# Rounding projected key blocks on ScalarE from PSUM instead of on VectorE from SBUF

## The chip, the cores and the metric

The kernel runs on one core of a Trainium2 chip. The metric is the device time of one execution in microseconds, from launch to end. The engines are called TensorE (PE in the profile; PEld is its weight load), VectorE (DVE), ScalarE (ACT), GpSimd (POOL) and SyncE (SP, which here only issues DMAs).

## What is computed

A layer norm, then causal attention with 16 heads plus a mixture of nine experts of which each token uses two, both added to the input. Cut to the attention, in which the change lies:

```
xn  = layernorm(x)                                  # x: 2 x 1024 x 128
K   = einsum('bpd,ihd->biph', xn, W_K)              # 16 heads of 64
Q   = einsum('bpd,ihd->biph', xn, W_Q)
V   = einsum('bpd,ihd->biph', xn, W_V)
s   = where(tril, einsum('biph,biqh->biqp', K, Q), -1e10)
z   = einsum('biph,biqp->biqh', V, softmax(s / 8))
out = x + einsum('bqf,df->bqd', z_flat, W_O) + moe(xn)
```

## The kernel before, in words

**Exactness.** TensorE multiplies in the type fp32r. To keep the accuracy of fp32, an operand is held as two fp32r tiles: the rounded value ("hi") and the remainder ("lo", the value less hi). A product is then two or three matmuls that accumulate. So nearly every matmul result goes through the same mill: ScalarE copies the PSUM bank into hi (a copy to an fp32r tile rounds), VectorE subtracts hi from the bank and writes lo.

**Stages.** The first 142 us hold the layer norm, the routing and the experts. Then come the attention's 16 halves: 8 pairs of heads (p), and for each the two sequences of the batch (b = 0, 1). A half has 16 score units, one for each head of the pair and each 128-row block of queries, in the order of `UNITS`: unit 0 has 1024 columns of keys, unit 1 has 128, unit 2 has 896, and so on. For each unit n these steps follow one another:

- S n, on PE (line 1390): scores into one half of `ps_big`, which two units share in turn. S n waits for the exponential of unit n-2.
- X n, on DVE (line 1109): the mask and the row's maximum.
- E n, on ACT (line 853): the exponential into `probs`, with its sum, which a short second instruction (the accumulator read) delivers. Its end releases the bank.
- R n, on DVE (line 1147): the reciprocal of the sum. N n, on POOL (line 693): the division.
- T n.g, on PE (line 1422): transposes of up to four tiles into one of the two banks of `ps_mid`. H n.g, on ACT (line 866), makes hi of it, and L n.g, on DVE (line 1158), lo. T of a group waits for L of the group two before it.
- V, on PE (lines 1442 and 1443): probabilities times values into `ps_z` or `ps_big`, and Z, the moves and sums of that result.

**Projections.** While a half runs, the queries and keys of the next half are projected, and in 7 of the 15 halves that have a successor the values too. Each projection is an M on PE (lines 1252 to 1254) and a C on ACT and on DVE. All of them use one PSUM bank, `ps_misc`: an M waits until the previous user has read the bank. They come in the order k0, q0, q1, k1, then the values v0, v2, v3 where they are made, then the output product o1, and so on; k0 and k1 are the first and second 512 keys.

**Key blocks before the change.** For k0 and k1 (there are 30 such blocks in all, two in each of 15 halves; the very first keys are made another way) ACT copies the bank as it is into `part_raw` (line 764), which frees the bank. DVE then copies `part_raw` from SBUF to SBUF into the hi rows of the stack `k_st` of the next half (line 946), which rounds it. POOL later subtracts (line 704, `raw - hi`), and only after that SP moves the parts where the scores want them. POOL does this at K0 and K1, which stand behind N4 and N6 of the half.

**What sets the order.** Four tables written out by hand, `PE_ORDER`, `ACT_ORDER`, `DVE_ORDER` and `POOL_ORDER`, give each engine's order in a half; every engine runs strictly in that order, and counting semaphores tie them together. A "+" means that the entry belongs to the next half. Around the key blocks they read, on ACT, "E14 Ck0+ H11.0 E15 H12.0 Z1 H12.1 E0+ H13.0 E1+ Cq0+" and "E5 H2.1 Ck1 E6 H3.0 Cv0 H4.0 E7"; on DVE "R14 Ck0+ L11.0 X0+ R15 L12.0 X1+ L12.1 Z1 L13.0 X2+ R0+" and "X7 R5 Ck1 R6 L3.0 Cv0 X8"; on PE "S15 V3.1 Mk0+ T11.0 T12.0 S0+ Mq0+ T12.1 V4.0 S1+ V4.1 T13.0 S2+ T14.0 T14.1" and "S6 T2.1 Mk1 V7.0- S7 T3.0 Mv0 T4.0 S8".

The names that the prediction uses: `proj_filled` (PE has filled `ps_misc`), `proj_copied` (ACT has copied it; for keys this frees the bank), `part_rounded` (DVE has rounded a key block), `pool_split` (POOL has its lo), `s_ready` (a score unit is in PSUM).

Of the kernel before, what the change touches and what calls it, by code (L numbers as in the profile page):

```python
# [20 lines left out]
def bass_layernorm_causal_attention_plus_moe_kernel(  # L21
# [47 lines left out]
    with ExitStack() as ctx:  # L69
# [6 lines left out]
        def sem(name):  # L76
            return ctx.enter_context(nc.semaphore(name))
# [165 lines left out]
        hid_done = sem("hid_done"); down_done = sem("down_done")  # L243
        pads_zero = sem("pads_zero"); down_zero = sem("down_zero")
        proj_filled = sem("proj_filled"); proj_copied = sem("proj_copied"); proj_split = sem("proj_split")
        part_rounded = sem("part_rounded"); pool_split = sem("pool_split")
        stacked = {name: sem(f"stacked_{name}") for name in ("q0", "q1", "k0", "k1")}
        moved = {name: sem(f"moved_{name}") for name in ("k0", "k1")}
        s_ready = sem("s_ready"); max_done = sem("max_done"); exp_done = sem("exp_done")
# [113 lines left out]
        def pooled_count(p, b, name):  # L363

            return 4 * p + 2 * b + [n for n in MISC_ORDER if n[0] == "k"].index(name) + 1
# [227 lines left out]
        def _(pool):  # L593
# [105 lines left out]

            def split_part(p, b, name):  # L700

                pool.wait_ge(part_rounded, pooled_count(p, b, name))
                raw, hi, lo = part_views(name, 1 - b)
                pool.tensor_tensor(lo, raw, hi.bitcast(F32), ALU.subtract).then_inc(pool_split, 1)  # L704

# [23 lines left out]
        def _(act):  # L729
# [20 lines left out]
            def copy_proj(p, b, name, bank=ps_misc[:, :]):  # L750
                b_next = 1 - b
                act.wait_ge(proj_filled, proj_count(p, b, name))
                if name[0] == "q" and p >= 0:
                    act.wait_ge(stacked[name], 64 * (2 * p + b + 1))
                if name == "wqkv":
                    nc.scalar.activation(w_hi[:, 0, :], bank[:, 0:P], ACT.Copy, scale=-DH ** -0.5)
                    n = 4 if p % 2 else 2
                    ins = nc.scalar.activation(w_hi[:, 1:n, :], bank[:, P:n * P].rearrange("p (m r) -> p m r", m=n - 1), ACT.Copy)
                elif name == "wo":
                    ins = nc.scalar.activation(wo_hi[:], bank[:, 0:P], ACT.Copy)  # L760
                elif name[0] in POOLED and p >= 0:
                    c = int(name[1])
                    wait(act, pool_split, pooled_count(p, b, name) - 2)
                    ins = nc.scalar.activation(part_raw[c][:], bank, ACT.Copy)
                elif name[0] in "qk":
                    c = int(name[1])
                    dst = q_parts if name[0] == "q" else k_parts
                    ins = nc.scalar.activation(dst[:, 0, c * BLK:(c + 1) * BLK], bank, ACT.Copy)
                else:
                    tiles = slice(2 * int(name[1]), 2 * int(name[1]) + 2)  # L770
                    if p >= 0:
                        wait(act, pv_done, 8 * (2 * p + b))
                    ins = nc.scalar.activation(v_st[b_next][:, tiles, :, 0, :],
                                               bank.rearrange("p (t h c) -> p t h c", t=2, h=4), ACT.Copy)
                ins.then_inc(proj_copied, 1)
# [155 lines left out]
        def _(dve):  # L931
# [7 lines left out]

            def split_proj(p, b, name, bank=ps_misc[:, :]):  # L940
                b_next = 1 - b
                dve.wait_ge(proj_copied, proj_count(p, b, name))
                if name[0] in POOLED and p >= 0:
                    dve.wait_ge(s_ready, UPH * (2 * p + b))
                    raw, hi, _ = part_views(name, b_next)
                    nc.vector.tensor_copy(hi, raw).then_inc(part_rounded, 1)
                    return
                if name == "wqkv":
                    nc.vector.scalar_tensor_tensor(out=w_lo[:, 0, :], in0=bank[:, 0:P], scalar=-DH ** -0.5,
                                                   in1=w_hi[:, 0, :].bitcast(F32), op0=ALU.mult, op1=ALU.subtract)  # L950
# [629 lines left out]
```

## Time and profile before

| | |
|---|---|
| time, median of 3 runs | 688.08 us (687.35 to 690.8) |
| the profiled execution, its own time | 690.95 us |
| its span, first to last instruction | 689.1 us |
| mean granted TensorE clock | 0.981 of 2.4 GHz |
| busy: PE / PEld | 664.0 us (96%) / 598.8 us (87%) |
| busy: DVE / ACT / POOL | 613.6 us (89%) / 543.3 us (79%) / 484.7 us (70%) |
| chain that ended last | PE 67%, DVE 6%, POOL 3%, ACT 1% |

The times of the views are from the profiled execution, which is 2.87 us above the median of the runs. 1.85 us of it lie around its span. A timeline row gives the start, the duration, the engine, the line, the tiles (written <- read), and in brackets the idle time of the engine before it with what ended that. The duration runs until the result has landed; the next instruction of the same engine can start a little before that.

### The profile page before, as it was taken

The page shows a single profiled execution, that of the slowest core. Times are in us where ns is not written, and L with a number is a line of the kernel's source. Part 1 is how long each engine was busy: PE and PEld are TensorE (multiplying, and loading weights), DVE is VectorE, ACT ScalarE, POOL GpSimd, SP SyncE. Part 2 cuts the span into 40 slices and gives each one's busy share as a digit, 9 for nine tenths or more (in the row PEclk, how much of TensorE's full clock was granted, in tenths as well). Part 3 has the DMA queues.
Part 4 walks back from the last instruction along what each step waited for, and adds up shares of the span by engine and source line. Part 5 has one row for each costly group of instructions (what it writes and reads, how often), then busy time and mean ns, then how long its engine had stood idle before and what let it go on. Part 6 is the DMA issues. An engine that isn't in the chain of part 4 may idle for free.

```text
span 689.1 us, 14712 instructions
## 1 busy us (share of the span) xinstructions
PE 664.0 (96%) x4589; PEld 598.8 (87%) x4589; DVE 613.6 (89%) x1657; ACT 543.3 (79%) x1280; POOL 484.7 (70%) x494
## 2 busy tenths in 40 slices
PE   8879999979999999999999999999999999999996
PEld 7759999968988899998888999988889999897886
DVE  8886777668999999999999999999999999998996
ACT  4744555568988888898898989888889898888873
POOL 5273444247796878787977878687978686979861
PEclk9878999999999999999999999999999999999999
DMA  7524642216060616151624343334526150616001
GB/s 229 162 60 94 151 109 58 40 32 156 10 158 23 158 26 144 31 135 32 146 69 98 75 95 81 85 83 95 121 46 137 32 142 25 142 32 159 7 27 36
DMA packets 50235, 61.01 MB, mean 89 GB/s; under 512 B 7440, under 2 KB 28272, under 8 KB 50160
## 3 DMA queue, kind: packets, MB, share of 16 engines
q1 hardware_dynamic: 47856, 55.36, 33.5%
q0 software_dynamic: 2304, 4.72, 2.9%
q8 instruction: 39, 0.64, 0.4%
q14 instruction: 36, 0.29, 0.1%
HBM read 12.87 MB, written 4.72 MB: 26 GB/s over the span
## 4 chain that ended last, share of the span: by engine, by line
PE 67%; DVE 6%; POOL 3%; ACT 1%; issue 1%; ACTq 0%
PE ps_big L1390 18%; PE ps_mid L1422 17%; PE ps_z L1443 7%; PE ps_z L1442 7%; PE ps_misc L1252 5%; PE ps_misc L1254 4%; PE ps_misc L1253 4%; PE ps_big L1443 3%; PE ps_big L1442 3%; DVE ps_big L1109 2%; DVE pT_lo L1158 2%; POOL probs L693 1%; POOL z_lo L698 1%; POOL k_st L704 1%; DVE z_sum L1166 1%
## 5 line engine op out<-in xcount | busy, mean ns | idle before, releaser
L693 POOL TENSOR_TENSOR probs<-probs,rden 128x1024 f32<-128x1024 f32 (+7 forms) x256 | 294.0, 1164 | 98.1 <-DVE rden L1147 96.9
L866 ACT ACTIVATE pT_hi<-ps_mid 128x512 fp32r<-128x512 f32 (+3 forms) x384 | 184.3, 493 | 54.7 <-PE ps_mid L1422 50.4
L1158 DVE TENSOR_TENSOR pT_lo<-ps_mid,pT_hi 128x512 fp32r<-128x512 f32 (+3 forms) x384 | 206.8, 550 | 10.4 <-ACT pT_hi L866 7.8
L1109 DVE CUSTOM_DVE_ANT_0 ps_big<-ps_big,later 128x1024 f32<-128x1024 f32 (+7 forms) x256 | 194.3, 759 | 11.9 <-PE ps_big L1390 9.7
L1390 PE MATMUL ps_big<-k_st,q_st 128*128 128x512 f32 (+2 forms) x768 | 194.0, 364 | 0.4 <-issue 0.2
L853 ACT ACTIVATE probs<-ps_big,neg_max 128x1024 f32<-128x1024 f32 (+7 forms) x256 | 190.1, 743 | 4.3 <-DVE neg_max L1109 3.5
L1422 PE MATMUL ps_mid<-ident,probs 128*128 128x128 f32 x1152 | 180.2, 276 | 5.5 <-DVE pT_lo L1158 4.0
L1422 PEld LDWEIGHTS ps_mid<-ident,probs 128*128 128x128 f32 x1152 | 132.4, 141 | 27.2 <-issue 13.9
L1390 PEld LDWEIGHTS ps_big<-k_st,q_st 128*128 128x128 f32 x768 | 125.0, 190 | 13.6 <-ACT probs L853 2.0
L1442 PE MATMUL ps_z<-pT_hi,v_st 128*128 128x256 f32 x448 | 116.5, 291 | 0.0
L1443 PE MATMUL ps_z<-pT_lo,v_st 128*128 128x256 f32 x448 | 112.9, 282 | 0.0
L1443 PEld LDWEIGHTS ps_z<-pT_lo,v_st 128*128 128x128 f32 x448 | 85.0, 190 | 1.4
L1442 PEld LDWEIGHTS ps_z<-pT_hi,v_st 128*128 128x128 f32 x448 | 84.6, 189 | 1.4
L645 POOL DMA_INDIRECT xg<-xn_dram,tok_i x40 | 39.8, 996 | 47.4 <-PE ps_misc L1329 46.0
L853 ACT ACTIVATION_READ_ACCUMULATOR probs<-ps_big,neg_max 128x1 f32 x256 | 52.6, 205 | 0.0
L1442 PE MATMUL ps_big<-pT_hi,v_st 128*128 128x256 f32 x192 | 51.1, 288 | 0.0
L1443 PE MATMUL ps_big<-pT_lo,v_st 128*128 128x256 f32 x192 | 49.7, 281 | 0.0
L826 ACT ACTIVATE silu<-ps_big 128x352 f32<-128x352 f32 x40 | 18.6, 464 | 33.8 <-PE ps_big L1349 33.8
L698 POOL TENSOR_TENSOR z_lo<-z_sum,z_hi 128x512 fp32r<-128x512 f32 x30 | 38.7, 1291 | 4.4 <-ACT z_hi L882 4.4
L1147 DVE RECIPROCAL rden<-den 128x1 f32<-128x1 f32 x256 | 39.5, 155 | 0.4 <-ACT probs L853 0.3
L704 POOL TENSOR_TENSOR k_st<-part_raw,k_st 128x512 fp32r<-128x512 f32 x30 | 38.8, 1292 | 0.0
L1443 PEld LDWEIGHTS ps_big<-pT_lo,v_st 128*128 128x128 f32 x192 | 36.3, 189 | 2.0
(242 smaller groups left out, 1222.9 us busy)
## 6 DMA issues: line engine op xcount, KB each, us to landing
k_st<-k_st SPq DMA_DIRECT2D x90, 256.0 KB, 3.6
q_st<-q_parts SPq DMA_DIRECT2D x128, 128.0 KB, 3.1
y_dram<-y_sb SPq DMA_DIRECT2D x40, 64.0 KB, 1.7
k_st<-k_parts SPq DMA_DIRECT2D x8, 256.0 KB
raw_gu<-in_L_ffn_Wg_dram SPq DMA_DIRECT2D x9, 176.0 KB, 3.0
raw_gu<-in_L_ffn_Wu_dram SPq DMA_DIRECT2D x9, 176.0 KB, 3.1
raw_d<-in_L_ffn_Wd_dram SPq DMA_DIRECT2D x9, 128.0 KB, 3.1
res<-in_L_attn_x_dram SPq DMA_DIRECT2D x4, 256.0 KB, 3.6
```

The source lines that it names most:

```text
L645: pool.indirect_dma_start(xg[n % 4][:], None, xn_dram, bass.IndirectOffsetOnAxis(tok_i[:, n:n + 1], 0)).then_inc(xg_in[n % 4], 16)
L693: pool.tensor_tensor(rows, rows, col.to_broadcast([P, width]), ALU.mult).then_inc(normed, 1)
L698: pool.tensor_tensor(z_lo[j][:], z_sum[j][:], z_hi[j][:].bitcast(F32), ALU.subtract).then_inc(zlo_done, 1)
L704: pool.tensor_tensor(lo, raw, hi.bitcast(F32), ALU.subtract).then_inc(pool_split, 1)
L853: nc.scalar.activation(probs[n % 4][:, 0:width], ps_big[:, n % 2, off:off + width], ACT.Exp, bias=neg_max[:, n:n + 1], scale=-1.0, accum_o ...
L866: nc.scalar.activation(pT_hi[:, t:t + 2 * tiles - 1:2, :], ps_mid[:, bank, 0:tiles * P].rearrange("p (t q) -> p t q", t=tiles), ACT.Copy). ...
L1109: nc.vector.tensor_tensor_reduce(cols, cols, later[:, S - width:S], 1.0, FLOOR, ALU.add, ALU.min, neg_max[:, n:n + 1]).then_inc(max_done, 1)
L1158: nc.vector.tensor_tensor(pT_lo[:, at, :], ps_mid[:, bank, 0:tiles * P].rearrange("p (t q) -> p t q", t=tiles), pT_hi[:, at, :].bitcast(F3 ...
L1390: ins = nc.tensor.matmul(ps_big[:, n % 2, c0:c1], w, k_st[half][h][:, part, c0 - off:c1 - off], start=part == 0, stop=part == 1, skip_grou ...
L1422: ins = nc.tensor.transpose(ps_mid[:, bank, c * P:(c + 1) * P], probs[n % 4][:, kt * P:(kt + 1) * P], ident[:])
L1442: nc.tensor.matmul(dst, w, pT_hi[:, at, :], start=kt == 0, stop=False, skip_group_check=True)
L1443: ins = nc.tensor.matmul(dst, w, pT_lo[:, at, :], start=False, stop=kt == tiles - 1, skip_group_check=True)
```

## The change

For the 30 key blocks, ACT now issues two instructions in a row where it issued one: the plain copy of the bank into `part_raw`, and a second read of the same bank that writes the rounded block straight into `k_st`. `proj_copied` is raised by the second of them. The instruction of DVE at line 946 goes, with its two waits and its semaphore `part_rounded`. The wait that protects the stack (all scores of the half before have been issued) now stands on ACT between the two copies. POOL waits for `proj_copied` where it waited for `part_rounded`. The order tables are untouched.

```
             def split_part(p, b, name):
-                pool.wait_ge(part_rounded, pooled_count(p, b, name))
+                pool.wait_ge(proj_copied, proj_count(p, b, name))
                 raw, hi, lo = part_views(name, 1 - b)
                 pool.tensor_tensor(lo, raw, hi.bitcast(F32), ALU.subtract).then_inc(pool_split, 1)
...
                 elif name[0] in POOLED and p >= 0:
-                    c = int(name[1])
+                    raw, hi, _ = part_views(name, b_next)
                     wait(act, pool_split, pooled_count(p, b, name) - 2)
-                    ins = nc.scalar.activation(part_raw[c][:], bank, ACT.Copy)
+                    nc.scalar.activation(raw, bank, ACT.Copy)
+                    act.wait_ge(s_ready, UPH * (2 * p + b))
+                    ins = nc.scalar.activation(hi, bank, ACT.Copy)
...
             def split_proj(p, b, name, bank=ps_misc[:, :]):
                 b_next = 1 - b
+                if name[0] in POOLED and p >= 0:
+                    return
                 dve.wait_ge(proj_copied, proj_count(p, b, name))
-                if name[0] in POOLED and p >= 0:
-                    dve.wait_ge(s_ready, UPH * (2 * p + b))
-                    raw, hi, _ = part_views(name, b_next)
-                    nc.vector.tensor_copy(hi, raw).then_inc(part_rounded, 1)
-                    return
```

On ACT, at key block k0 of a half in the middle of the attention, this stood before (E14, the raw copy, H11.0, E15, H12.0, the move Z1, H12.1, E0 of the next half):

```order
L853 ACTIVATE probs,den<-ps_big,neg_max 128x1024 [waits t_ready,max_done]
L764 ACTIVATE part_raw<-ps_misc 128x512 [waits pool_split,proj_filled]
L866 ACTIVATE pT_hi<-ps_mid 128x3x128 [waits t_ready]
L853 ACTIVATE probs,den<-ps_big,neg_max 128x128 [waits t_ready,max_done]
L866 ACTIVATE pT_hi<-ps_mid 128x4x128 [waits t_ready,pv_done]
L876 ACTIVATE z_sum<-ps_big 64x512 [waits zlo_done,pv_done]
L866 ACTIVATE pT_hi<-ps_mid 128x3x128 [waits t_ready]
L853 ACTIVATE probs,den<-ps_big,neg_max 128x1024 [waits t_ready,max_done]
```

And this stands there now, two lines further down in the file from the second copy on:

```order
L855 ACTIVATE probs,den<-ps_big,neg_max 128x1024 [waits t_ready,max_done]
L764 ACTIVATE part_raw<-ps_misc 128x512 [waits pool_split,proj_filled]
L766 ACTIVATE k_st<-ps_misc 128x512 [waits s_ready]
L868 ACTIVATE pT_hi<-ps_mid 128x3x128 [waits t_ready]
L855 ACTIVATE probs,den<-ps_big,neg_max 128x128 [waits t_ready,max_done]
L868 ACTIVATE pT_hi<-ps_mid 128x4x128 [waits t_ready,pv_done]
L878 ACTIVATE z_sum<-ps_big 64x512 [waits zlo_done,pv_done]
L868 ACTIVATE pT_hi<-ps_mid 128x3x128 [waits t_ready]
L855 ACTIVATE probs,den<-ps_big,neg_max 128x1024 [waits t_ready,max_done]
```

One instruction of the size of the raw copy has come in behind it; everything else on ACT keeps its place. On DVE, at the same place of the program, this stood before (Z0 of the half, R14, the rounding, L11.0, X0 of the next half with its accumulator read, R15, L12.0):

```order
L1166 TENSOR_TENSOR z_sum<-ps_z,z_sum 64x512 [waits z_moved]
L1147 RECIPROCAL rden<-den 128x1 [waits exp_done]
L946 CAST k_st<-part_raw 128x512 [waits s_ready,proj_copied]
L1158 TENSOR_TENSOR pT_lo<-ps_mid,pT_hi 128x3x128 [waits pT_copied]
L1109 ISA ps_big,neg_max<-ps_big,later 128x1024 [waits s_ready]
L1109 ISA neg_max 128x1
L1147 RECIPROCAL rden<-den 128x1 [waits exp_done]
L1158 TENSOR_TENSOR pT_lo<-ps_mid,pT_hi 128x4x128 [waits pT_copied]
```

And this stands there now:

```order
L1165 TENSOR_TENSOR z_sum<-ps_z,z_sum 64x512 [waits z_moved]
L1146 RECIPROCAL rden<-den 128x1 [waits exp_done]
L1157 TENSOR_TENSOR pT_lo<-ps_mid,pT_hi 128x3x128 [waits pT_copied]
L1108 ISA ps_big,neg_max<-ps_big,later 128x1024 [waits s_ready]
L1108 ISA neg_max 128x1
L1146 RECIPROCAL rden<-den 128x1 [waits exp_done]
L1157 TENSOR_TENSOR pT_lo<-ps_mid,pT_hi 128x4x128 [waits pT_copied]
```

The rounding copy is gone and nothing has taken its place; R14 is now followed by L11.0. PE, POOL and SP have the same instructions in the same order.

## Rows read from the trace of the kernel before

**Rows 1.** The page's busy times of all engines, with their counts of instructions.

```profile
PE 664.0 (96%) x4589; PEld 598.8 (87%) x4589; DVE 613.6 (89%) x1657; ACT 543.3 (79%) x1280; POOL 484.7 (70%) x494
```

**Rows 2.** Busy time by stretch, one half: PE, PEld, DVE, ACT, POOL, clock, DMA.

```profile
405.80:439.20 33.40, 33.40 (x239) 30.49 (x238) 32.12 (x85) 29.98 (x71) 26.55 (x26) 1.00 0.36 86
```

**Rows 3.** Waits from 140 to 650 us: who waited for whom, us, times, longest.

```profile
PEld ps_mid L1422 <- POOL probs L693: 3.5, 10, 1.0
...
PEld ps_big L1390 <- ACT probs L853: 1.6, 8, 0.2
...
PEld ps_misc L1252 <- ACT part_raw L764: 1.2, 1, 1.2
```

**Rows 4.** Groups of instructions by form: the two copies of a key block.

```profile
L764 ACT ACTIVATE part_raw<-ps_misc 128x512 f32<-128x512 f32 x30 | 18.1, 602 | 2.3 <-PE ps_misc L1254 2.1
...
L946 DVE CAST k_st<-part_raw 128x512 fp32r<-128x512 f32 x30 | 12.5, 418 | 1.8 <-issue 1.8
```

**Rows 5.** Timeline of all engines around key block k0 of one half.

```profile
407.02 0.61 ACT L764 ACTIVATE part_raw<-ps_misc 128x512 f32<-128x512 f32 x1
...
407.36 1.17 PE L1390 MATMUL ps_big<-k_st,q_st 128*128 128x512 f32 x4
407.50 0.51 ACT L866 ACTIVATE pT_hi<-ps_mid 128x384 fp32r<-128x384 f32 x1
...
407.66 0.43 DVE L946 CAST k_st<-part_raw 128x512 fp32r<-128x512 f32 x1
407.78 2.06 POOL L693 TENSOR_TENSOR probs<-probs,rden 128x1024 f32<-128x1024 f32 x1 [1.44 <-DVE rden L1147]
...
408.05 0.56 DVE L1158 TENSOR_TENSOR pT_lo<-ps_mid,pT_hi 128x384 fp32r<-128x384 f32 x1
...
408.57 1.23 DVE L1109 CUSTOM_DVE_ANT_0 ps_big<-ps_big,later 128x1024 f32<-128x1024 f32 x1
...
409.98 1.11 ACT L853 ACTIVATE probs<-ps_big,neg_max 128x1024 f32<-128x1024 f32 x1
...
410.98 0.20 ACT L853 ACTIVATION_READ_ACCUMULATOR probs<-ps_big,neg_max 128x1 f32 x1
...
411.23 0.76 PEld L1390 LDWEIGHTS ps_big<-k_st,q_st 128*128 128x128 f32 x4
...
413.49 0.67 DVE L960 TENSOR_TENSOR q_parts<-ps_misc,q_parts 128x512 fp32r<-128x512 f32 x1
...
413.66 1.90 POOL L693 TENSOR_TENSOR probs<-probs,rden 128x1024 f32<-128x1024 f32 x1 [2.56 <-DVE rden L1147]
...
414.22 0.19 PEld L1252 LDWEIGHTS ps_misc<-xT_hi,w_hi 128*128 128x128 f32 x1
```

**Rows 6.** The same view around key block k1 of a half that makes values.

```profile
421.45 0.60 ACT L764 ACTIVATE part_raw<-ps_misc 128x512 f32<-128x512 f32 x1
...
422.49 0.19 PEld L1252 LDWEIGHTS ps_misc<-w_hi,xT_hi 128*128 128x128 f32 x1
...
423.51 0.60 ACT L773 ACTIVATE v_st<-ps_misc 128x512 fp32r<-128x512 f32 x1 [0.33 <-PE ps_misc L1254]
```

**Rows 7.** The same view around key block k1 of a half without values.

```profile
455.87 0.60 ACT L764 ACTIVATE part_raw<-ps_misc 128x512 f32<-128x512 f32 x1
...
457.04 0.20 ACT L853 ACTIVATION_READ_ACCUMULATOR probs<-ps_big,neg_max 128x1 f32 x1
...
457.56 0.65 PEld L1390 LDWEIGHTS ps_big<-k_st,q_st 128*128 128x128 f32 x4
...
462.05 1.30 POOL L698 TENSOR_TENSOR z_lo<-z_sum,z_hi 128x512 fp32r<-128x512 f32 x1
...
463.42 0.19 PEld L1252 LDWEIGHTS ps_misc<-z_hi,wo_hi 128*128 128x128 f32 x1 [0.38 <-issue]
```

**Rows 8.** Line 693 alone, two stretches: durations in ns (min/median/max), starts, forms.

```profile
L693 POOL TENSOR_TENSOR probs<-probs,rden x2: 828/1148/1467, 435.6 to 437.0; 128x768 f32<-128x768 f32 x1, 128x384 f32<-128x384 f32 x1
...
L693 POOL TENSOR_TENSOR probs<-probs,rden x1: 920/920/920, 457.8 to 457.8; 128x384 f32<-128x384 f32 x1
```

More of the change, by code:

```diff
@@ L245, in bass_layernorm_causal_attention_plus_moe_kernel @@
         proj_filled = sem("proj_filled"); proj_copied = sem("proj_copied"); proj_split = sem("proj_split")
-        part_rounded = sem("part_rounded"); pool_split = sem("pool_split")
+        pool_split = sem("pool_split")
         stacked = {name: sem(f"stacked_{name}") for name in ("q0", "q1", "k0", "k1")}
```

## The prediction

> **What bounds the kernel now.** I read the page's busy times first [rows 1], then the busy times of single halves of the attention [rows 2], then the waits [rows 3], and last the timeline around the places that the change touches [rows 5 to 7]. In a half of 33.40 us PE is busy for all 33.40 us at the full granted clock (1.00, so 2.4 GHz), VectorE for 32.12 and ScalarE for 29.98 us [rows 2]. A busy PE is not proof, since its matmuls overlap, but the waits say the same: from 140 to 650 us the weight loads wait 3.5 us for GpSimd's divisions and 1.6 us for exponentials, none longer than 1.0 us [rows 3]. So PE's own stream of work sets the pace, the others keep just ahead of it, and what is left to gain by serving PE sooner is a few microseconds. What there is to lose is not bounded in that way: a delay of another engine that reaches PE is added to the time, because PE has no idle time later from which to take it back. So the question at each of the 30 key blocks is how much slack stands between ScalarE, which gets work, and PE.
>
> **What is removed.** 30 rounding copies on VectorE of 418 ns, 12.5 us in all [rows 4]. In a half these are two of 32.12 us of work. This work lies on no path at k0: VectorE rounds at 407.66, and L11.0 behind it starts at 408.05, which is 0.04 us after ScalarE's H11.0 ended (407.50 + 0.51 = 408.01) [rows 5]. Without the copy L11.0 would still have waited for H11.0. I take 0 for its removal there.
>
> **What is added.** 30 ScalarE copies from the same bank in the same shape as the raw copy, 602 ns each [rows 4]. The next instruction starts before such a copy has ended: H11.0 follows the raw copy by 407.50 - 407.02 = 0.48 us [rows 5]. So each costs ScalarE's queue 0.48 us and holds the bank that much longer; 30 x 0.48 = 14.4 us of ScalarE's time. The moved wait (all scores of the half before issued) costs nothing: on PE the S15 that satisfies it stands before Mk0, which the raw copy has already waited for, and for k1 it is half a half old. What remains is where the 0.48 us go, and that differs between k0 and k1.
>
> **Key block k0 (14 places in the steady attention).** Queued behind the added copy are H11.0, E15, H12.0, Z1, H12.1, E0+. H11.0 then ends at 408.49 instead of 408.01, L11.0 starts at 408.53 instead of 408.05, and VectorE, being in order, starts X0+ 0.52 us later, at 409.05 instead of 408.57. Before, X0+ started 0.04 us after its scores ended (407.36 + 1.17 = 408.53) [rows 5], so PE had released it at the moment at which VectorE was free: slack of about 0.04 us. From X0+ on the chain has no gap: E0+ starts at 409.98 when the maximum is there, its accumulator read ends at 410.98 + 0.20 = 411.18, and PE's first weight load for S2+, which needs that bank, starts at 411.23, 0.05 us later [rows 5]. So PE gets S2+ about 0.44 us later. A little comes back: Mq1's weight load at 414.22 already waits for VectorE's q lo (413.49 + 0.67 = 414.16) [rows 5]. That instruction follows X2+ and so also moves, but by 0.06 us less than PE, since X2+ had that much slack behind its scores. Net 0.38 us at this place. I read the other 13 places in the same view, in the same way: the slack of VectorE ahead of X0+ is 0.05 to 0.49 us there, 0.15 on average, because the ends of E14 and T11.0 fall a little differently from half to half. Net over the 14 places: 0.48 - 0.15 - 0.06 = 0.27 us each, **3.8 us**. The bounds: 14 x 0 = 0, if an idle moment swallows it that I don't see, and 14 x 0.48 = 6.7 us.
>
> The bank itself is no matter at k0: the second copy would end at 408.1, and Mq0, which needs the bank, stands behind S0+, whose weight loads and matmuls run to about then.
>
> **The first half (one k0, one k1).** At the attention's start PE does wait for the raw copy, 1.2 us, once [rows 3]; there the bank's later release is PE's delay in full. I charge 0.48 us for it and, without a row of its own, nearly as much for the k1 of the same half, which is as tight: **0.9 us**, between 0.5 and 1.0.
>
> **Key block k1, halves with values (6 more).** The bank is asked for soon: Mv0's weight load starts at 422.49 and the raw copy ended at 421.45 + 0.60 = 422.05 [rows 6]. With 0.05 us for the semaphore, as at S2+, the slack is 0.39 us, so 0.09 us reach PE. On ScalarE 0.33 us of idle time ahead of the copy of v0 [rows 6] take up part, and 0.48 - 0.33 = 0.15 us go on through a queue that from there to the next M's has no idle time. I take 0.15: **0.9 us**, between 0.5 and 2.9 (6 x 0.48).
>
> **Key block k1, halves without values (8).** No M follows soon. What follows is E6, whose accumulator read ends at 457.04 + 0.20 = 457.24, and S8, which needs it and loads weights at 457.56 [rows 7]: slack 0.32 less 0.05, so S8 comes 0.2 us late. But further on PE waits anyway: the weight load of the output product o1 at 463.42 had 0.38 us of idle time before it and starts when GpSimd's z lo is done (462.05 + 1.30 = 463.35) [rows 7]. The 0.2 us vanish in that wait. And that wait gets shorter: GpSimd's queue runs without a gap from N5, at 457.83, to this z lo, and N5 ran beside the rounding copy. A division of 1024 columns takes 2.06 us beside one and 1.90 us without [rows 5]; one of 384 columns took 920 ns beside one (at 457.8) and 828 ns without (at 437.0) [rows 8]. So z lo comes 0.09 us sooner: 8 x 0.09 = **0.7 us gained**, between 0 and 1.4 (8 x 0.17). At k0 the same gain of 0.16 us is worth nothing, since GpSimd idles 2.56 us soon after [rows 5].
>
> On why a GpSimd instruction is longer beside the rounding copy, the Trainium skill has a rule: in "SBUF — State Buffer", section "Who interferes with whom", VectorE in a two-port mode and GpSimd share a port pair as an exclusive lock, and the second to issue blocks until the first has finished. By that, the division at 407.78 would have lost all of the 0.31 us that the copy still ran, and the trace shows 0.16: so the direction agrees and the size is about half. If the rule held in full at k1, the gain there would be 8 x 0.23 = 1.8 us instead of 0.7, and the sum 3.8 instead of 4.9 us.
>
> **The sum.** 3.8 + 0.9 + 0.9 - 0.7 = 4.9 us slower. Against the profiled execution's own time: 690.95 + 4.9 = 695.9 us, of which 694.0 us are span. That execution is 2.87 us above the median of the runs, and I forecast the median: 688.08 + 4.9 = **693.0 us**, 0.7% above before.
>
> **The rivals.**
> *Absorbed (about 689.2 us).* ScalarE is idle for 3.4 of 33.4 us in a half [rows 2], and PE's order may give S2+ more room than I read, since without its wait it could have started only about 0.06 us sooner. Then k0 costs nothing and the rest is 0.9 + 0.9 - 0.7 = 1.1 us: 688.08 + 1.1. Against it: the 0.05 us between the accumulator read and the weight load, which says that the wait binds.
> *All of it on the path (about 697 to 702 us).* If each late step makes the next one later, the k0 places cost their 6.7 us, the k1 places of both kinds 14 x 0.2 to 0.48 = 2.8 to 6.7 us, the first half 1.0: 10.5 to 14.4 us. The z lo wait speaks against it in 8 halves.
> *VectorE sets the pace, and the kernel gets faster (about 682 us).* VectorE is busy 32.12 of 33.40 us [rows 2]. If it were the true bound at k1, each of 15 rounding copies there would give back the 0.39 us from its start to that of the next instruction (407.66 to 408.05 [rows 5]): 5.9 us. This would need ScalarE to keep H3.0 ahead of VectorE. By my count H3.0 comes 0.48 us later, which is more than the 0.39 us that VectorE gains, so nothing is left; the point from which this rival decides is an added step on ScalarE of less than 0.39 us.
> That the change does not do what it says can be left out: the order of the instructions shows the copy gone from VectorE and added on ScalarE.
>
> **How the numbers follow.** Forecast (sum with its bounds, 691 to 697 us) 0.60; absorbed 0.22; all on the path 0.11; faster 0.07. The range runs from just below the absorbed case, 688.8, to inside the third, 699.0, and leaves out the faster case and about half of the third. About 0.5% (3.4 us) is what a measurement of this kernel can tell from no change. Slower by more: nine tenths of the forecast and all of the third case, 0.66. Within: the rest of the forecast and nearly all of the absorbed case, 0.28. Faster: 0.06.
>
> **What the profile of the changed kernel would show.** ScalarE busy for about 561 us (543.3 + 30 x 0.6), VectorE for about 601 us. At k0: L11.0 starts 0.04 us after a later H11.0, X0+ starts some 0.5 us after its scores end instead of 0.04, and the wait of the scores' weight loads for exponentials grows from 1.6 us to several. GpSimd's 1024-column divisions would all take 1.90 us. At k1 of halves without values S8 waits 0.2 us and o1 waits less than 0.38. I am wrong if X0+ still starts 0.04 us after its scores (then H11.0 was not late, or VectorE was), if PE's wait at S2+ grows but the half stays at 33.4 us (then PE takes it back somewhere), or if the added copy moves H11.0 by other than 0.48 us.

## The result

The changed kernel takes 692.96 us in the median of 14 runs (690.56 to 697.03). The kernel before takes 687.81 us in the median of 14 runs that stand beside them. The ratio is 1.0074 with a 95% interval from 1.0054 to 1.0094, so the change costs 0.7%, or between 3.7 and 6.5 us. The forecast was 693.0 us and slower.

The page of the changed kernel has these busy times of the engines, in the form of [rows 1]:

```profile
PE 662.4 (96%) x4589; PEld 593.1 (86%) x4589; DVE 605.0 (88%) x1627; ACT 556.6 (81%) x1310; POOL 480.9 (70%) x494
```

30 instructions left VectorE and 30 came to ScalarE. ScalarE is busy 13.3 us more than in [rows 1] and VectorE 8.6 us less.

One caution comes before any comparison of spans. The two profiled executions ran at different mean clocks: 0.981 for the kernel before, whose span is 689.1 us, and this for the one after:

```profile
core 0: 688.4 us, clock 0.990
```

Its span is shorter although the kernel is slower, because its stretch ahead of the attention had more clock. I therefore compare a stretch in which the granted clock was 1.00 in both: from the second raw copy of a k0 block to the last one, 13 halves. The rows of ScalarE at its two ends are, first of the kernel before:

```profile
174.71 0.61 ACT L764 ACTIVATE part_raw<-ps_misc 128x512 f32<-128x512 f32 x1
...
606.70 0.61 ACT L764 ACTIVATE part_raw<-ps_misc 128x512 f32<-128x512 f32 x1
```

and of the kernel after:

```profile
170.63 0.61 ACT L764 ACTIVATE part_raw<-ps_misc 128x512 f32<-128x512 f32 x1
...
605.68 0.61 ACT L764 ACTIVATE part_raw<-ps_misc 128x512 f32<-128x512 f32 x1
```

That is 431.99 us before and 435.05 us after: 3.06 us more in 13 halves. Below I call this the steady stretch, and give it for every experiment. It comes from one trace of each kernel, and it is not free of chance: ahead of the first scores of a half (S0+) PE sometimes waits up to 0.4 us for the last part of the keys to land by DMA. In the half whose k0 starts at 206.60 before and at 202.70 after, only the kernel before has such a wait (0.43 us); from k0 to k1 that half takes 14.87 us before and 14.79 after, and 14.77 in e2 against 14.90 in e6, two of the experiments below. So differences of 0.4 us in the steady stretch say nothing.

**Key block k0 after the change.** The timeline around the place of [rows 5]. Times there are read from the start of the raw copy, 404.32 here and 407.02 in [rows 5]:

```profile
404.32 0.61 ACT L764 ACTIVATE part_raw<-ps_misc 128x512 f32<-128x512 f32 x1
...
404.65 1.18 PE L1389 MATMUL ps_big<-k_st,q_st 128*128 128x512 f32 x4
404.80 0.62 ACT L766 ACTIVATE k_st<-ps_misc 128x512 fp32r<-128x512 f32 x1
...
405.07 1.89 POOL L693 TENSOR_TENSOR probs<-probs,rden 128x1024 f32<-128x1024 f32 x1 [1.45 <-DVE rden L1146]
405.27 0.52 ACT L868 ACTIVATE pT_hi<-ps_mid 128x384 fp32r<-128x384 f32 x1
...
405.82 0.56 DVE L1157 TENSOR_TENSOR pT_lo<-ps_mid,pT_hi 128x384 fp32r<-128x384 f32 x1 [0.83 <-ACT pT_hi L868]
...
406.30 1.22 DVE L1108 CUSTOM_DVE_ANT_0 ps_big<-ps_big,later 128x1024 f32<-128x1024 f32 x1
406.44 0.31 PEld L1421 LDWEIGHTS ps_mid<-ident,probs 128*128 128x128 f32 x3 [0.35 <-DVE pT_lo L1157]
406.44 0.55 PE L1421 MATMUL ps_mid<-ident,probs 128*128 128x128 f32 x3
406.65 0.59 ACT L878 ACTIVATE z_sum<-ps_big 64x512 f32<-64x512 f32 x1
...
407.27 0.49 ACT L868 ACTIVATE pT_hi<-ps_mid 128x384 fp32r<-128x384 f32 x1
...
407.44 0.14 DVE L1108 DVE_READ_ACCUMULATOR2_ANT neg_max<- 128x1 f32 x1
...
407.66 1.11 ACT L855 ACTIVATE probs<-ps_big,neg_max 128x1024 f32<-128x1024 f32 x1
...
408.65 0.20 ACT L855 ACTIVATION_READ_ACCUMULATOR probs<-ps_big,neg_max 128x1 f32 x1
...
408.91 0.76 PEld L1389 LDWEIGHTS ps_big<-k_st,q_st 128*128 128x128 f32 x4 [0.27 <-ACT probs L855]
...
411.85 0.19 PEld L1251 LDWEIGHTS ps_misc<-xT_hi,w_hi 128*128 128x128 f32 x1
```

| step | before [rows 5], us after the raw copy | after | later by |
|---|---|---|---|
| H11.0 on ScalarE | 0.48 | 0.95 | 0.47 |
| L11.0 on VectorE | 1.03 | 1.50 | 0.47 |
| X0+ on VectorE | 1.55 | 1.98 | 0.43 |
| H12.1 on ScalarE, just ahead of E0+ | 2.58 | 2.95 | 0.37 |
| E0+ on ScalarE | 2.96 | 3.34 | 0.38 |
| weight load of S2+ | 4.21 | 4.59 | 0.38 |
| weight load of Mq1 | 7.20 | 7.53 | 0.33 |

VectorE now sits idle 0.83 us ahead of L11.0, in the time that its rounding copy used to fill. X0+ starts 0.47 us after its scores end (404.65 + 1.18 = 405.83), where it was 0.04 us. The division on GpSimd takes 1.89 instead of 2.06 us, which helps nobody here.

One more thing stands in these rows. E0+ starts 0.38 us behind H12.1 before and 0.39 us behind it after, so it is ScalarE's queue that it follows. These are the rows of the kernel before that [rows 5] leaves out, the last transposes of T12.1, H12.1 and the end of X0+:

```profile
409.07 0.49 PE L1422 MATMUL ps_mid<-ident,probs 128*128 128x128 f32 x3
...
409.60 0.49 ACT L866 ACTIVATE pT_hi<-ps_mid 128x384 fp32r<-128x384 f32 x1
...
409.72 0.14 DVE L1109 DVE_READ_ACCUMULATOR2_ANT neg_max<- 128x1 f32 x1
```

Before, H12.1 starts 0.04 us after the transposes end (409.07 + 0.49 = 409.56), at all 14 places of k0: ScalarE waits there for PE. After, it starts 0.28 us after them (406.44 + 0.55 = 406.99; 0.21 to 0.29 us at 13 of the 14) and directly behind the move Z1 (406.65 + 0.59 = 407.24): ScalarE has had no idle time since the raw copy. The row maximum, which comes over L11.0 and X0+, is there 0.12 us before E0+ in the kernel before and 0.08 us before it now. So two roads lead from the added copy to E0+: ScalarE's own queue, and the way over VectorE. They arrive almost together, and e10 below tells which of them is enough.

**Key block k1 of a half that makes values**, to be set beside [rows 6]:

```profile
419.07 0.60 ACT L764 ACTIVATE part_raw<-ps_misc 128x512 f32<-128x512 f32 x1
...
419.57 0.59 ACT L766 ACTIVATE k_st<-ps_misc 128x512 fp32r<-128x512 f32 x1
...
420.21 0.19 PEld L1251 LDWEIGHTS ps_misc<-w_hi,xT_hi 128*128 128x128 f32 x1
...
421.23 0.60 ACT L775 ACTIVATE v_st<-ps_misc 128x512 fp32r<-128x512 f32 x1
```

Mv0's weight load comes 1.14 us after the raw copy (1.04 before), and the copy of v0 2.16 us after it (2.06 before), with its idle time of 0.33 us gone: 0.10 us late.

**Key block k1 of a half without values**, beside [rows 7]:

```profile
453.91 0.60 ACT L764 ACTIVATE part_raw<-ps_misc 128x512 f32<-128x512 f32 x1
...
455.56 0.21 ACT L855 ACTIVATION_READ_ACCUMULATOR probs<-ps_big,neg_max 128x1 f32 x1
...
460.02 1.28 POOL L698 TENSOR_TENSOR z_lo<-z_sum,z_hi 128x512 fp32r<-128x512 f32 x1
...
461.37 0.19 PEld L1251 LDWEIGHTS ps_misc<-z_hi,wo_hi 128*128 128x128 f32 x1 [0.28 <-issue]
```

The accumulator read is 1.65 us behind the raw copy (1.17 before), and S8's first weight load is at 455.82, so 1.91 us behind (1.69 before): S8 is 0.22 us late. The product o1 is 7.46 us behind (7.55 before), so 0.09 us *early*: the lateness vanished in its wait for z lo, and z lo itself came sooner.

**The waits** from 135 to 655 us, beside [rows 3]:

```profile
PEld ps_big L1389 <- ACT probs L855: 5.7, 26, 0.3
...
PEld ps_misc L1251 <- ACT k_st L766: 2.1, 2, 1.7
```

The wait of the scores for exponentials grew from 1.6 us in 8 places to 5.7 us in 26. The bank's wait in the first half grew from one of 1.2 to one of 1.7 and one of 0.4 us.

### The profile page after: what moved, and what is told of

Same layout as the page of the kernel before. It is cut to its first block, busy times and chain, and to the rows that moved or that the text cites. A ratio compares the mean times of both kernels' runs of the same rounds, so it can differ in the third digit from the quotient of the medians.

```text
span 688.4 us, 14683 instructions
## 1 busy us (share of the span) xinstructions
PE 662.4 (96%) x4589; PEld 593.1 (86%) x4589; DVE 605.0 (88%) x1627; ACT 556.6 (81%) x1310; POOL 480.9 (70%) x494
## 4 chain that ended last, share of the span: by engine, by line
PE 83%; DVE 6%; issue 4%; ACT 4%; POOL 2%; DMA 1%; SPq 0%; POOLq 0%; ACTq 0%; DVEq 0%
PE ps_big L1389 19%; PE ps_mid L1421 17%; PE ps_z L1442 7%; PE ps_z L1441 7%; PE ps_misc L1251 5%; PE ps_misc L1253 4%; PE ps_misc L1252 4%; PE ps_big L1442 3%; PE ps_big L1441 3%; PE ps_big L1346 3%; PE ps_z L1371 2%; PE ps_z L1372 2%; PE ps_mid L1357 2%; PE ps_big L1347 2%; PE ps_big L1348 2%
## 5 line engine op out<-in xcount | busy, mean ns | idle before, releaser
L693 POOL TENSOR_TENSOR probs<-probs,rden 128x1024 f32<-128x1024 f32 (+7 forms) x256 | 290.2, 1148 | 103.6 <-DVE rden L1146 102.3
```

The source lines that it names most:

```text
L693: pool.tensor_tensor(rows, rows, col.to_broadcast([P, width]), ALU.mult).then_inc(normed, 1)
```

## The experiments

The theory from the prediction: the loss is made at k0, where 0.48 us are put between the raw copy and H11.0 on ScalarE, and reaches PE at S2+ over VectorE's X0+; k1 is nearly neutral; the 14.4 us of load on ScalarE cost nothing as such, and the 12.5 us taken off VectorE bring nothing. The rivals: the load on ScalarE costs wherever it stands; VectorE's relief pays; or the cost is the longer hold of the bank. What I call worked out by place is the difference of matmul start times between two traces, one record against its counterpart, from one key block to the next.

In the diffs `BY_ACT` names the blocks that ScalarE rounds. The times of e1 to e4 stand beside 688.82 us, the median of 23 runs of the kernel before on their chip; those of the other four beside 689.73 us, again 23 runs.

### One key block alone

**e1_k0_only** changes k0 and leaves k1 as before (`BY_ACT = "k0"`; the last two lines are VectorE's, which makes no copy for that block).

```
+                    ins = nc.scalar.activation(raw, bank, ACT.Copy)
+                    if name == BY_ACT:
+                        act.wait_ge(s_ready, UPH * (2 * p + b))
+                        ins = nc.scalar.activation(hi, bank, ACT.Copy)
...
+                if name == BY_ACT and p >= 0:
+                    return
```

> Only key block k0 is rounded by ScalarE from PSUM; k1 stays with VectorE. Queue theory (mine): the cost sits at k0, where the added copy makes H11.0 late and, through VectorE's order, X0+, E0+ and S2+. From the start of one k0 to the next, the halves lengthen by 0.17 to 0.38 us, 3.6 us in the 14 steady halves; with some 0.5 us in the first half, 4 to 4.5 us slower than before (about 692). The weight loads of the scores wait for exponentials 5 to 6 us instead of 1.6. Load theory (rival): each added ScalarE copy costs the same wherever it stands, so half the copies cost half: 2.5 us slower (690.3). Bank theory (rival): the longer hold of the bank is what costs; at k0 Mq0 is late, which the trace would show as a wait of Mq0's weight load, and S2+ is late only by that.

Measured: 695.09 us in 6 runs, ratio 1.0094 (1.0073 to 1.0115). The steady stretch takes 435.21 us, 3.22 more than before, and the 14 places of k0 worked out one by one give 3.5 us. The median is 3 us above the forecast of 692, and the trace does not bear that out. Most of these six executions had little clock: the two with a mean clock of 0.988 took 692.0 and 693.4 us, against 688.0 to 688.8 us of the kernel before at 0.988. At equal clock that is 4 to 5 us.

**e2_k1_only** is the same with `BY_ACT = "k1"`.

> Only key block k1 is rounded by ScalarE from PSUM; k0 stays with VectorE. Queue theory: 6 halves with values cost 0.09 us each (the bank), 8 without gain 0.1 us each (o1 waits less for GpSimd's z lo), and the first half loses 0.9 us: +0.5 - 0.9 + 0.9 = 0.5 us slower, which runs cannot tell from nothing (688.4). Load theory: 2.5 us slower (690.3). VectorE-sets-the-pace theory: 15 copies less on VectorE give back 0.39 us each, 5.9 us faster (682).

Measured: 688.63 us in 12 runs, ratio 1.0006 (0.9984 to 1.0028). The steady stretch takes 431.55 us, 0.44 less. The waits of the scores for exponentials, first of e1, then of e2, where k0 is as before:

```profile
PEld ps_big L1399 <- ACT probs L860: 5.0, 21, 0.3
```

```profile
PEld ps_big L1399 <- ACT probs L860: 2.3, 13, 0.2
```

So the loss is k0's: k1 by itself costs nothing that the runs can tell. e2 also answers the rival by which VectorE sets the pace: with half of its rounding copies gone, where the forecast put that rival's gain, the time is the same. The two runs' changes in the steady stretch add up to 2.8 us, the whole change to 3.06, which is the same within 0.4.

### Load or place

**e5_late_both** and **e6_late_k0** give ScalarE the rounding, but later in its order, from `part_raw` in SBUF (the steps G0 and G1), so that the raw copy alone frees the bank and H11.0 follows it as before.

```
-            H14.0- H14.1- E2 H15.0- Cq1 E3 H0.0 H0.1 E4 H1.0 Z2- H2.0 E5 H2.1 Ck1 E6 H3.0 Cv0 H4.0 E7 Z3- H4.1
+            H14.0- H14.1- E2 G0 H15.0- Cq1 E3 H0.0 H0.1 E4 H1.0 Z2- H2.0 E5 H2.1 Ck1 E6 H3.0 G1 Cv0 H4.0 E7 Z3- H4.1
...
+            def round_key(p, b, name):
+                raw, hi, _ = part_views(name, 1 - b)
+                act.wait_ge(proj_copied, proj_count(p, b, name))
+                act.wait_ge(s_ready, UPH * (2 * p + b))
+                nc.scalar.activation(hi, raw, ACT.Copy).then_inc(part_rounded, 1)
```

e6 has G0 only, and k1 as before.

> ScalarE rounds both key blocks, but later, from part_raw in SBUF: k0 behind E2 of the next half, where ScalarE had 0.47 us of idle time ahead of H15.0, and k1 behind H3.0. The raw copy frees the bank at once, as before. ScalarE gets the same 30 instructions as in the change, VectorE loses the same 30. A copy from SBUF of this size took 0.64 us and pushes ScalarE's queue by 0.65 us (z hi in the trace of before). Queue theory: at k0 0.2 us are left over and nothing of it binds PE; at k1 the copy of v0 comes 0.3 us late in the halves with values, and in the others o1 still waits 0.09 us less: between 1 us faster and 2 us slower than before (688 to 690). Load theory: it costs what the change costs, 5 us (693), or more, as the copies are longer.

> Only k0 is rounded late by ScalarE from SBUF, behind E2 of the next half; k1 stays with VectorE. Queue theory: the 3.6 us that the k0 places cost in the change are gone, X0+ starts 0.04 us after its scores again; within 1 us of before (688.5). Load theory: 15 copies more, 2.5 us slower or more (691). GpSimd's 1024-column division at k0 takes 1.90 us, for no gain.

Measured: e5 689.75 us in 12 runs, ratio 0.9994 (0.9973 to 1.0014), steady stretch 431.60 us (0.39 less than before). e6 689.19 us in 12 runs, ratio 0.9999 (0.9981 to 1.0018), steady stretch 432.26 us (0.27 more). The durations of the moved copy, minimum, median and maximum in ns, in e5:

```profile
L782 ACT ACTIVATE k_st<-part_raw x30: 622/634/642, 149.6 to 623.4; 128x512 fp32r<-128x512 f32 x30
```

e5 gives ScalarE the same 30 copies, each a little longer (634 ns from SBUF, against 602 from PSUM), takes the same 30 from VectorE, and costs nothing. The load theory falls: some 14 us of added work on an engine that is busy 29.98 of 33.40 us in a half [rows 2] is free at one place of its order, and costs the whole 0.7% at another. In e5 the moved copy starts 7.7 to 8.1 us after the raw copy at k0 and 1.6 to 1.7 us after it at k1. VectorE's relief is worth nothing that these runs can tell either.

### Which road at k0

**e10_hi_behind_H11** puts the second copy from PSUM one step later, behind H11.0, so that H11.0 is not held up, but the bank is.

```
-            H10.1 E14 Ck0+ H11.0 E15 H12.0 Z1 H12.1 E0+ H13.0 E1+ Cq0+""")
+            H10.1 E14 Ck0+ H11.0 G0+ E15 H12.0 Z1 H12.1 E0+ H13.0 E1+ Cq0+""")
```

> The changed kernel with ScalarE's second copy of k0 one place later, behind H11.0, still from the bank. H11.0, L11.0 and X0+ are then on time; the bank is held until about 1.46 us after the raw copy began instead of 1.1. Queue theory: what was waited for at S2+ comes back at Mq0 (its weight load waits some 0.4 us for the bank), and E15 to E0+ are as late as in the change, so it costs as much as the change or a little more: 693 to 694. If H11.0's lateness alone were the cost, this kernel would be back at some 689.

Measured: 693.05 us in 6 runs, ratio 1.0064 (1.0039 to 1.0089), steady stretch 435.04 us, 3.05 more than before: the same cost as the change itself. Its timeline at the same k0, with the raw copy at 406.78:

```profile
407.25 0.51 ACT L875 ACTIVATE pT_hi<-ps_mid 128x384 fp32r<-128x384 f32 x1
...
407.62 0.63 ACT L784 ACTIVATE k_st<-ps_misc 128x512 fp32r<-128x512 f32 x1
407.80 0.56 DVE L1166 TENSOR_TENSOR pT_lo<-ps_mid,pT_hi 128x384 fp32r<-128x384 f32 x1 [0.34 <-ACT pT_hi L875]
...
408.30 0.19 PEld L1260 LDWEIGHTS ps_misc<-xT_hi,w_hi 128*128 128x128 f32 x1 [0.45 <-ACT k_st L784]
...
408.33 1.23 DVE L1117 CUSTOM_DVE_ANT_0 ps_big<-ps_big,later 128x1024 f32<-128x1024 f32 x1
...
409.10 0.49 PE L1430 MATMUL ps_mid<-ident,probs 128*128 128x128 f32 x3
...
409.48 0.14 DVE L1117 DVE_READ_ACCUMULATOR2_ANT neg_max<- 128x1 f32 x1
...
409.73 0.49 ACT L875 ACTIVATE pT_hi<-ps_mid 128x384 fp32r<-128x384 f32 x1
...
410.11 1.11 ACT L862 ACTIVATE probs<-ps_big,neg_max 128x1024 f32<-128x1024 f32 x1
```

H11.0 is where it was, 0.47 us behind the raw copy, and X0+ is at 1.55 us, as before. So the way over VectorE is clear: the row maximum is ready 0.49 us before E0+. Yet E0+ starts 3.33 us after the raw copy, where it was 2.96 before and 3.34 in the change, again 0.38 us behind H12.1. Nor is it PE that H12.1 waits for: its transposes ended 0.14 us before it (409.10 + 0.49 = 409.59). At 13 of the 14 places it is 3.32 to 3.34. ScalarE's own queue, without VectorE, is therefore enough to make E0+, and S2+ behind it (4.58 us, against 4.59 in the change), as late as the change does.

The bank has no room either: PE waits 0.45 us for it ahead of Mq0, whose weight load comes 1.52 us after the raw copy instead of 1.12. What the longer hold would cost with E0+ on time, no run shows, because here both come together. In the change itself the bank was free just in time: the second copy ended at 404.80 + 0.62 = 405.42, and Mq0's weight load follows at 405.46, 1.14 us after the raw copy against 1.12 before.

### The two edits apart, and a miss

**e4_removed_only** leaves out the raw copy: ScalarE makes one copy, with rounding, and VectorE none. GpSimd's subtraction then has no raw rows to read, so it subtracts the hi rows from themselves, and the lo parts of the projected keys are zero.

```
-                    ins = nc.scalar.activation(part_raw[c][:], bank, ACT.Copy)
+                    act.wait_ge(s_ready, UPH * (2 * p + b))
+                    ins = nc.scalar.activation(hi, bank, ACT.Copy)
...
-                pool.tensor_tensor(lo, raw, hi.bitcast(F32), ALU.subtract).then_inc(pool_split, 1)
+                pool.tensor_tensor(lo, hi.bitcast(F32), hi.bitcast(F32), ALU.subtract).then_inc(pool_split, 1)
```

> VectorE's rounding copy is gone and ScalarE's queue is as long as before: ScalarE makes one copy, from PSUM straight into the rounded block, and the raw copy is left out; GpSimd subtracts the rounded block from itself, so the lo part of keys 30 blocks is zero (part of the computation is left out, and its time is that of the change without the added copy). Queue theory: nothing is late, o1 waits 0.09 us less in 8 halves: 0 to 1 us faster than before (687). VectorE-sets-the-pace theory: 30 x 0.39 = 11.7 us of VectorE's queue come back, at least 5 us faster (under 683).

Measured: 686.6 us in 12 runs, ratio 0.9971 (0.9952 to 0.999), steady stretch 429.36 us, 2.63 less than before. Its median is 2.2 us below the kernel before. By place, k0 changes nothing, and each k1 of a half without values gains 0.35 us. The reason is mostly in the experiment, not in the change: with one source tile the subtraction is shorter. Line 704 in e4, then in the changed kernel:

```profile
L704 POOL TENSOR_TENSOR k_st<-k_st x30: 1032/1042/1050, 151.9 to 621.1; 128x512 fp32r<-128x512 f32 x30
```

```profile
L704 POOL TENSOR_TENSOR k_st<-part_raw,k_st x30: 1272/1294/1310, 150.8 to 626.5; 128x512 fp32r<-128x512 f32 x30
```

0.25 us of the 0.35 are this, and 0.09 the division without the rounding copy beside it. So e4 overstates what the removal is worth, and what remains for the removal itself is those 0.09 us. It does show one thing cleanly: GpSimd's queue is what o1 waits for.

**e3_added_only** does ScalarE's second copy and keeps VectorE's rounding copy too (both write the same rounded rows, VectorE later).

```
-                    ins = nc.scalar.activation(part_raw[c][:], bank, ACT.Copy)
+                    nc.scalar.activation(raw, bank, ACT.Copy)
+                    act.wait_ge(s_ready, UPH * (2 * p + b))
+                    ins = nc.scalar.activation(hi, bank, ACT.Copy)
```

> Both: ScalarE's second copy is added as in the change, and VectorE's rounding copy stays too (it rounds the same block once more). It separates what the addition costs from what the removal gives. Queue theory: the addition costs all that the change costs, 5.1 us, and what the removal gives is the 0.9 us by which z lo comes sooner in 8 halves: 6 us slower than before (693.9). If the removal gave more (VectorE short of time), this kernel is slower than the changed one by as much: at 30 x 0.39 us it would be near 704. If the removal gave nothing, it equals the changed kernel (693).

Measured: 710.56 us in 6 runs, ratio 1.0339 (1.0309 to 1.0368), steady stretch 452.42 us, 20.43 more than before. Every theory missed this by far: 1.57 us in each half instead of 0.3. The timeline at k0, raw copy at 414.18, shows why:

```profile
414.94 1.89 POOL L693 TENSOR_TENSOR probs<-probs,rden 128x1024 f32<-128x1024 f32 x1 [1.43 <-DVE rden L1149]
...
415.31 1.81 DVE L948 CAST k_st<-part_raw 128x512 fp32r<-128x512 f32 x1 [0.45 <-ACT k_st L766]
...
417.03 0.55 DVE L1160 TENSOR_TENSOR pT_lo<-ps_mid,pT_hi 128x384 fp32r<-128x384 f32 x1
```

The rounding copy takes 1.81 us where it took 0.43. What differs is the order of two starts. In [rows 5] the copy started at 407.66 and GpSimd's division at 407.78, 0.12 us later. Here the copy has to wait for a later signal from ScalarE (0.45 us idle) and starts 0.37 us *after* the division. It ends at 417.12, 0.29 us after the division's end at 416.83. All 14 copies at k0 that meet a 1024-column division show the same.

### A theory formed on the miss

Theory: the rounding copy and a division on GpSimd exclude one another, whichever starts first, and the copy needs the shared thing for 0.29 us. Rival: it is something that ScalarE's second copy does to the rounding copy in e3 (same destination, same time).

**e11_round_behind_L11** has no second copy on ScalarE. It is the kernel before with one pair of steps swapped on VectorE, so that the rounding copy starts behind L11.0 and thus after the division.

```
-            L8.1 R12 X13 L9.0 Cwo X14 R13 Cwqkv+ L10.0 L10.1 X15 Z0 R14 Ck0+ L11.0 X0+ R15 L12.0 X1+ L12.1 Z1
+            L8.1 R12 X13 L9.0 Cwo X14 R13 Cwqkv+ L10.0 L10.1 X15 Z0 R14 L11.0 Ck0+ X0+ R15 L12.0 X1+ L12.1 Z1
```

> The kernel before, with VectorE's rounding copy of k0 one place later, behind L11.0, so that it meets GpSimd's 1024-column division (which begins 0.12 us after the copy began in the trace of before) in mid course instead of just ahead of it. Nothing is added or removed. Lock theory, formed on the run in which both copies stood (there the copy took 1.81 us, from 415.31 to 417.12, beside a division from 414.94 to 416.83): the copy waits for the division's end, X0+ comes some 1.3 us late at each of 14 places, about 18 us slower (706). Queue theory alone: X0+ comes 0.39 us late less its slack of 0.15 on average: 3.5 us slower (691.5).

Measured: 703.63 us in 6 runs, ratio 1.0218 (1.0189 to 1.0247), steady stretch 445.77 us, 13.78 more than before. Timeline at k0, raw copy at 411.17:

```profile
411.93 1.89 POOL L693 TENSOR_TENSOR probs<-probs,rden 128x1024 f32<-128x1024 f32 x1 [1.45 <-DVE rden L1147]
...
412.19 0.56 DVE L1158 TENSOR_TENSOR pT_lo<-ps_mid,pT_hi 128x384 fp32r<-128x384 f32 x1 [0.34 <-ACT pT_hi L866]
...
412.67 1.44 DVE L946 CAST k_st<-part_raw 128x512 fp32r<-128x512 f32 x1
...
414.03 1.22 DVE L1109 CUSTOM_DVE_ANT_0 ps_big<-ps_big,later 128x1024 f32<-128x1024 f32 x1
```

The theory had foretold 706 us; each k0 place lost 1.1 us or so instead of 1.3. The copy ends at 414.11, again 0.29 us after the division's end (411.93 + 1.89 = 413.82). The rival falls, since ScalarE makes no second copy here. L11.0, which starts at 412.19 in the middle of the same division, takes its usual 0.56 us: it is this copy that is held up, not all of VectorE. Over the 30 copies, minimum, median and maximum in ns, e3 and then e11:

```profile
L948 DVE CAST k_st<-part_raw x30: 406/418/1826, 140.4 to 641.3; 128x512 fp32r<-128x512 f32 x30
```

```profile
L946 DVE CAST k_st<-part_raw x30: 405/419/1457, 141.4 to 634.7; 128x512 fp32r<-128x512 f32 x30
```

Only the 14 copies at k0 that meet such a division are long in either; the median is that of the others.

## Why the prediction was right, point by point

**What bounds the kernel.** Right: the loss shows as PE's wait at S2+, and the wait of the scores for exponentials grew as said, from 1.6 to 5.7 us.

**The removal at 0.** Right for VectorE, as far as e5 and e2 can tell. By its effect on GpSimd it is worth the 0.09 us at k1 that I charged.

**The addition at 0.48 us in ScalarE's queue.** Right: 0.47 us at H11.0.

**k0, 3.8 us.** Nearly right in size, and right in that the delay starts behind the added copy and reaches PE at S2+. The path between was read incompletely. I had E0+ start "when the maximum is there" and led the whole delay over L11.0 and X0+. But E0+ stood 0.38 us behind H12.1 before the change too, with the maximum 0.12 us old, and e10 has X0+ on time and E0+ as late as in the change. ScalarE's own queue carries the delay, with the way over VectorE arriving at the same moment. That my slack of 0.15 us, read at X0+, fits this queue as well is in part luck: both are waits for PE, of X0+ for its scores and of H12.1 for its transposes, and from place to place the two waits grow and shrink together. In the changed kernel E0+ starts 3.33 to 3.34 us after the raw copy at 13 of 14 places, wherever it was before.

Worked out by place the 14 lose 3.56 us. At the place of [rows 5] I forecast 0.44 us at S2+ and 0.38 net; it was 0.38 at S2+ and 0.33 net at Mq1. Of the 14 places 13 lost 0.17 to 0.34 us and one gained 0.08. That one is the half at 206.60, in which only the kernel before waited 0.43 us for keys by DMA; without this chance the 14 would have lost some 0.3 to 0.4 us more, an estimate from the other 13. I also missed a first step of the delay: T12.1's weight load waits 0.35 us for L11.0, and by place 0.13 of the 0.38 us arise there.

**The absorbed case.** The argument for it was that S2+, without its wait, could have started only about 0.06 us sooner. That is true and speaks for nothing: how little one gains by taking a wait away does not say how much one loses by adding to it.

**The first half, 0.9 us.** Right. The bank's waits there are 2.1 us against 1.2. The trace of before has 3.4 us at the lower clock in this half, but the experiments have none there: from the first raw copy to that of the next k0 it was 30.81 us in e4 and 30.87 in e5, 31.32 with k0 changed (e1), 31.26 with k1 changed (e2), and 31.76 in the changed kernel. So each block costs 0.4 to 0.5 us and both 0.9.

**k1 with values, 0.15 us each.** Oversized. The starts of the raw copies say 0.12: from k1 at 421.45 to the next k0 at 441.38 it was 19.93 us, and from 419.07 to 439.12 it is 20.05. By place 0.06 to 0.12 us, so some 0.6 us in all instead of 0.9. What reached PE was the bank's 0.10 us, for which I had 0.09, not the 0.15 us of ScalarE's queue.

**k1 without values, 0.09 us gained each.** Right: from k1 at 455.87 to the next k0 at 473.26 was 17.39 us, and from 453.91 to 471.21 it is 17.30. By place 0.08 to 0.12, or 0.8 us over the eight.

**The sum.** 3.6 + 0.9 + 0.6 - 0.8 = 4.3 us by the traces, where the forecast had 4.9. The medians say 5.15 us and their interval 3.7 to 6.5. Of the 0.9 us between, 0.37 us lie outside the span, first to last instruction, where I had charged nothing. An execution of the changed kernel takes 2.13 to 2.24 us more than its span, one of the kernel before 1.75 to 1.88 (46 executions). The same holds for the experiments: 2.12 to 2.24 in e4, e5 and e10, 1.75 to 1.85 in e1, e2, e3, e6 and e11. The long ones are the kernels in which VectorE rounds no key block of the 30; why that should lengthen the time around the span, no run shows. The remaining 0.5 us is no more than the DMA wait of the half at 206.60 and the noise can make. The match of the median to a tenth is luck; that the terms lie inside the interval is not.

**The signs.** L11.0 starts 0.03 us after a later H11.0, X0+ 0.47 us after its scores, and the 1024-column divisions take 1.89 to 1.91 us, as said. The busy times were forecast at 561 us for ScalarE and 601 for VectorE and came out at 556.6 and 605.0. I had added and taken off whole durations, but the records of neighbours overlap: the added copy starts 0.48 us after the raw copy, which is recorded with 0.61.

**The variant sum of 3.8 us.** Here my reading failed, though it moved the sum by little. The Trainium skill says in "SBUF — State Buffer", section "Who interferes with whom", that VectorE in a two-port mode and GpSimd hold a shared port pair exclusively and that the second to issue is blocked until the first has finished. The prediction set against it that the division had lost 0.16 of 0.31 us, and called the size about half. e3 and e11 show the blocking in full, 0.42 us grown to 1.46 and 1.83, as the rule has it. The 0.16 us agree too if the copy holds the ports for 0.29 us rather than for its recorded 0.43, an estimate from e3 and e11: from 407.66 to 407.95, and the division that started at 407.78 loses 0.17. At k1 the same working gives 0.12 us, and 0.09 were seen:

```profile
457.66 0.41 DVE L946 CAST k_st<-part_raw 128x512 fp32r<-128x512 f32 x1
```

```profile
457.83 0.92 POOL L693 TENSOR_TENSOR probs<-probs,rden 128x384 f32<-128x384 f32 x1 [1.03 <-DVE rden L1147]
```

My mistake was to take the end of a recorded duration as the end of what it holds. The variant sum of 3.8 us, which rested on 0.23 us at k1, was wrong for the same reason; the row was the better guide to the size, the rule to the mechanism, and only the mechanism could have foretold e3.

**The rivals.** All on the path: no, k1 has a wait in every half without values, as said. Its low end was also added up wrongly: 688.08 + 10.5 = 698.6 us, not 697. VectorE sets the pace: no (e2, e5).

No version beats the kernel before by what it computes; e5 and e6 equal it. GpSimd's queue ahead of o1 is where e4 found 2.6 us in the steady stretch, and how to have them with the lo parts kept was not tried.

## What to carry to other kernels

When several engines are nearly full, ask of a moved instruction which one stands behind it and how much slack lies between that one and PE, not how much idle time the receiving engine has: the same copies cost 0.7% right behind the raw copy and nothing further down the order. Follow the delay down the engine's own queue first, and over other engines second; here the queue alone was enough. Before a copy on VectorE is pushed later by even half a microsecond, see whether a GpSimd instruction starts in that gap; here that turned 0.42 us into 1.8. And compare spans only over stretches of equal granted clock, and look at the time outside the span too.

## What the hardware showed that I had not expected

A VectorE rounding copy of 128x512 from SBUF to SBUF took 1.81 us (e3) and 1.44 us (e11) instead of 0.42 when a GpSimd division had started 0.37 or 0.74 us before it, and it ended 0.29 us after the division both times, at all 14 places; a `tensor_tensor` on VectorE with one source in PSUM (L11.0 in e11) ran at its usual 0.56 us during such a division. The kernel before escapes this by 0.12 or 0.13 us at each of the 14 k0 places, which the changed kernel no longer needs to.

A GpSimd subtraction of 128x512 took 1.04 us when both sources were the same rows, and 1.29 us with two different tiles.

Two executions of one program differed by up to 6.5 us (690.56 to 697.03), and their mean granted clocks by 0.980 to 0.993; those of the changed kernel at 0.980 took 695.8 and 697.0 us, those at 0.990 from 690.6 to 692.3.

The time outside the span was 1.75 to 1.88 us in the kernels in which VectorE rounds key blocks and 2.12 to 2.24 us in those in which it rounds none, in every execution whose span is recorded (89 and 44 of them).
